# A reordered stage border, and token lists by one-hot products instead of scatters, in a scan layer with a top-1 expert layer behind it

## The reference

```
x = x + scan_layer(layernorm(x))
    dt    = softplus((x Wdt1^T) Wdt2^T + b)
    A_bar = exp(dt * A)                      # per token, column and state n
    B_bar = (A_bar - 1) / A * x * B_t[n]
    h     = A_bar * h + B_bar                # along the tokens
    y     = sum over n of h * C_t[n],  + D_skip * x
x = x + experts(layernorm(x))
    e   = argmax(softmax(x Wr + br))         # one of 8 per token
    out = gelu(x W1[e] + b1[e]) W2[e] + b2[e]
```

## Time and profile before

| | us |
|---|---|
| median of 3 runs | 740.08 (739.1 to 744.09) |
| the profiled execution, its own time | 739.52 |
| its span | 737.8 |
| PE busy | 683.1 (93%) |
| DVE busy | 545.9 (74%) |
| ACT busy | 470.5 (64%) |
| POOL busy | 472.8 (64%) |

### The profile page before, as it was taken

How to read it: one execution, slowest core, us unless ns; L and a number is a source line. 1 busy time by engine, 2 the same in 40 slices (tenths; PEclk the granted TensorE clock), 3 DMA queues, 4 the chain that set the end, 5 groups by cost and what they waited for, 6 DMA issues and landing times.

```text
span 737.8 us, 17452 instructions
## 1 busy us (share of the span) xinstructions
PE 683.1 (93%) x5820; PEld 575.8 (78%) x5821; DVE 545.9 (74%) x968; ACT 470.5 (64%) x983; POOL 472.8 (64%) x595
## 2 busy tenths in 40 slices
PE   8799899999998997997997887999999999999997
PEld 7677677787787776776776777889899999987776
DVE  5899999989999989998999997786433333344441
ACT  3986998998998987887895585322323233323451
POOL 3789988988969887899998684043324343333331
PEclk9699999999999998999999999999999999999999
DMA  7967843343242523372475379221111111211010
GB/s 241 303 205 266 270 153 83 114 149 115 89 140 92 152 86 104 67 142 87 85 148 60 74 215 310 82 65 44 52 56 51 54 56 45 64 31 39 26 44 14
DMA packets 43216, 82.46 MB, mean 112 GB/s; under 512 B 5368, under 2 KB 13565, under 8 KB 43136
## 3 DMA queue, kind: packets, MB, share of 16 engines
q1 hardware_dynamic: 38016, 68.84, 32.8%
q0 software_dynamic: 5120, 12.60, 5.7%
HBM read 69.49 MB, written 13.51 MB: 112 GB/s over the span
## 4 chain that ended last, share of the span: by engine, by line
PE 60%; ACT 13%; POOL 11%; issue 10%; DVE 3%; DMA 1%; DVEq 1%; POOLq 0%; ACTq 0%; SPq 0%
PE WW L1176 15%; PE misc L1213 15%; PE WW L1053 11%; POOL w_sb L667 7%; PE YY L1091 7%; ACT w_sb L842 5%; ACT Csb L832 5%; PE misc L1208 2%; PE WW L1170 2%; PE misc L971 2%; POOL b_sb L648 2%; PE misc L983 1%; DMA xin<-x_in 1%; PE YY L1139 1%; ACT xin L812 1%
## 5 line engine op out<-in xcount | busy, mean ns | idle before, releaser
L667 POOL TENSOR_TENSOR w_sb<-w_sb,Csb 128x512 f32<-128x512 f32 x202 | 255.3, 1275 | 53.2 <-DVE w_sb L1307 45.7
L1053 PE MATMUL WW<-b_sb,xin 64*128 64x130 f32 (+2 forms) x2304 | 202.3, 292 | 27.8 <-DVE w_sb L1307 14.5
L1053 PEld LDWEIGHTS WW<-b_sb,xin 64*128 64x128 f32 x2304 | 167.9, 191 | 74.7 <-issue 36.1
L1307 DVE TENSOR_TENSOR_SCAN w_sb<-WW,hlast,w_sb 128x512 f32<-128x512 f32 x152 | 187.6, 1268 | 7.0 <-PE WW L1053 4.2
L842 ACT ACTIVATE w_sb<-dt,negA 128x512 f32<-128x512 f32 x256 | 169.6, 709 | 8.4 <-DVE w_sb L1307 5.8
L918 ACT ACTIVATE dt<-WW,b1c 128x128 f32<-128x128 f32 x256 | 73.1, 387 | 137.0 <-PE WW L1176 132.5
L1091 PE MATMUL YY<-sm,w_sb 128*128 128x128 f32 x1024 | 143.0, 285 | 8.0 <-DVE row L1364 5.0
L740 POOL DMA_INDIRECT y_out<-CbX,ocol x36 | 42.2, 1171 | 157.8 <-DVE CbX L1732 153.4
L1091 PEld LDWEIGHTS YY<-sm,w_sb 128*128 128x128 f32 x1024 | 114.1, 144 | 22.8 <-issue 5.8
L1213 PE MATMUL misc<-w_sb,dt 128*128 x512 | 115.7, 379 | 0.4 <-issue 0.4
L832 ACT ACTIVATE Csb<-w_sb,invA 128x512 f32<-128x512 f32 x134 | 91.6, 713 | 28.9 <-POOL w_sb L667 28.7
(11 more groups left out here) (312 smaller groups left out, 828.1 us busy)
## 6 DMA issues: line engine op xcount, KB each, us to landing
w_sb<-c_rows SPq DMA_DIRECT2D x86, 256.0 KB, 4.0
CbX<-c_rows SPq DMA_DIRECT2D x42, 256.0 KB, 3.7
w_sb<-w_in SPq DMA_DIRECT2D x20, 512.0 KB, 6.4
token_rows<-row SPq DMA_DIRECT2D x8, 1024.0 KB, 4.9
w_sb<-w_in SPq DMA_DIRECT2D x24, 256.0 KB
xin<-x_in SPq DMA_DIRECT2D x8, 512.0 KB, 3.9
w_sb<-x_in SPq DMA_DIRECT2D x7, 512.0 KB, 7.8
b_sb<-b_in SPq DMA_DIRECT2D x1, 780.0 KB, 6.4
```

The source lines that it names most:

```text
L667: eng.tensor_tensor(hc[g % NHC], hb_of(g), Csb[i % NCS][:, :], ALU.mult).then_inc(s_hcp, 1)
L1053: return eng.matmul(to[:, a:a + width], x_rows[rows, k, h * P:(h + 1) * P], band[rows, k, at:at + width], start=start, stop=not start, ski ...
L1307: eng.tensor_tensor_scan(hb_of(g) if pooled(g) else w_of(g), w_of(g), A[g % NA], hlast[(q - 1) % 2][:, h * N + n:h * N + n + 1] if q % NC ...
```

## The change

It does three things.

1. VectorE's units change: in chunks 5 and 6 from 5, 8, 12 to 5, 12; in chunk 7 unit 13 becomes 15.
2. The early tiles' lists come from products of f32 marks. `mark_early(k)` writes two one-hot tiles for each of the 16 early tiles, 8 in chunk 5 and 8 in chunk 6, behind the scans of items 10, 12, ... 24. PE multiplies them in hops early0 (chunk 6) and early1 (chunk 7), in two halves each; `keep_half` and `keep_ids` store the sum. The scatters, the list in DRAM, its load and the hop `lists` are gone. `count` moves to the start.
3. The border is written in another order on DVE and PE, and ACT's first W1 copy moves into unit 12 of chunk 7.

The core of the diff:

```diff
-VECTOR_UNITS = [(1, 6, 9, 12)] + [(5, 8, 12)] * 6 + [(1, 4, 8, 10, 13)]
+VECTOR_UNITS = [(1, 6, 9, 12)] + [(5, 8, 12)] * 4 + [(5, 12)] * 2 + [(1, 4, 8, 10, 15)]
...
+        if q == NQ - 2:
+            at[1] = [("early0_a", q)] + at[1]
+            at |= {2: [("early0", q)]}
     else:
-        at = {1: [("cbt", q)], 3: [("u_a", q)], 4: [("u01", q), ("u23", q)], 6: [("lists", 0)],
+        at = {1: [("cbt", q)], 3: [("u_a", q)], 4: [("u01", q), ("u23", q)], 6: [("early1_a", q)], 7: [("early1", q)],
...
+        marks = w2_sb[:, 2 * H:4 * H].rearrange("p (j a c) -> p j a c", a=2, c=P)
...
                     if q == NQ - 1 and n == 9:
-                        load_lists()
-                    if 0 <= N * q + n - NB < 20:
+                        eng.wait_ge(s_full, HOP["early1", q] + 1)
+                        load_weights(18)
+                        load_weights(19)
+                    if 0 <= N * q + n - NB < 18:
...
-                    if q == NQ - 3 and n > 4 and n % 2:
-                        enlist(((n - 5) // 2,))
-                    if q == NQ - 2 and n % 2:
-                        enlist(((n + 11) // 2,))
-                    if last and n < 2:
-                        enlist((n + 14,))
...
+                    if last and n == 12:
+                        copy_first_W1()
...
-                elif name == "lists":
-                    eng.wait_ge(s_lists, 16 * (q + 1))
-                    for i in range(E * CAP // P):
-                        mm = eng.transpose(to[:, i * P:(i + 1) * P], lists_in[:, i * P:(i + 1) * P], ident)
+                elif name in ("early0", "early0_a", "early1", "early1_a"):
+                    group, half = int(name[5]), int(not name.endswith("_a"))
+                    for j in range(TI * half, TI * half + TI):
+                        eng.wait_ge(s_mark, 2 * TI * group + j + 1)
+                        mm = eng.matmul(to[:, 0:P], marks[:, j, 0, :], marks[:, j, 1, :], start=(j == 0),
+                                        stop=(j == 2 * TI - 1))
...
             def step(t, u, r):
-                if not (isinstance(t, int) and (t + 1 >= MT or t == 1)):
+                if not (isinstance(t, int) and (t + 1 >= MT or t in (1, 2))):
                     hidden(t + 1, (u + 1) % 4)
-                if not (isinstance(t, int) and t + 2 >= MT):
+                if not (isinstance(t, int) and (t + 2 >= MT or t == 1)):
                     turn_x(t + 2, (u + 2) % 4, r + (u + 2) // 4)
                 if isinstance(t, int) and t == 0:
+                    hidden(2, 2)
                     fill(*TAIL[0])
-                    hidden(2, 2)
-                    for hop in TAIL[1:5]:
+                    turn_x(3, 3, 0)
+                    for part in range(2):
+                        fill(*TAIL[1 + part])
+                        hidden(3, 3, (part,))
+                    for hop in TAIL[3:5]:
                         fill(*hop)
                         keep_warm(6)
+                outputs(t, u)
+                if isinstance(t, int) and t == 0:
                     fill("spread", 1)
-                outputs(t, u)
...
+            def mark_early(k):
+
+                if k == 2 * TI:
+                    eng.wait_ge(s_full, HOP["early0", NQ - 2] + 1)
+                j = k % (2 * TI)
+                eng.tensor_scalar(marks[:, j, 0, :], counted[:, 0:P], where[:, 0, k:k + 1], back[:, k:k + 1],
+                                  ALU.is_equal, ALU.mult)
+                eng.tensor_scalar(marks[:, j, 1, :].rearrange("p (e c) -> p e c", e=E),
+                                  counted[:, :].rearrange("p (e c) -> p e c", e=E)[:, :, 0:LEVELS],
+                                  where[:, 1, k:k + 1], None, ALU.is_equal).then_inc(s_mark, 1)
...
-                if batch == 0:
-                    eng.tensor_copy(slotu[:, :], slotf).then_inc(s_slot, 1)
-                    return
...
             def keep_ids():
 
-                eng.wait_ge(s_full, HOP["lists", 0] + 1)
-                eng.tensor_copy(ids[:, 0:E * CAP], spot("lists", 0)[:, 0:E * CAP]).then_inc(s_ids, 1)
+                eng.wait_ge(s_spread, 1)
+                eng.wait_ge(s_full, HOP["early1", NQ - 1] + 1)
...
+            def keep_half():
+
+                eng.wait_ge(s_full, HOP["early0", NQ - 2] + 1)
+                eng.tensor_scalar(listed0, spot("early0", NQ - 2)[:, 0:P], FAR, None, ALU.add).then_inc(s_spread, 1)
...
+                    if q in (NQ - 3, NQ - 2) and gap and j in range(10, 26, 2):
+                        mark_early((q - NQ + 3) * 2 * TI + (j - 10) // 2)
+                    if q == NQ - 2 and (j, gap) == (5, 0):
+                        keep_half()
...
             copy_W1(1, 1)
-            for part in range(4):
-                choose(1, part)
+            copy_W1(2, 2)
+            choose(1, 0)
             q = NQ - 1
             for i in range(2):
                 finish_rows(q, i)
             for i in range(2):
                 ln2_stats(i, q)
             aggregate(1, q)
-            eng.wait_ge(s_ids, 1)
-            count()
+            copy_xT(2, 2)
+            for part in range(1, 4):
+                choose(1, part)
+            copy_W1(3, 3)
+            copy_xT(3, 3)
...
                 if isinstance(t, int) and t == 0:
                     place_tokens(1)
+                    mark(1, range(0, 6))
                     logits(NQ - 1)
+                    mark(1, range(6, 12))
                     for part in range(4):
                         choose(2, part)
                     join(1)
```

108 lines of the change are left out of this document (51 added, 57 removed).

## The result

The changed kernel takes 745.5 us (median of 7 runs, 743.65 to 749.9), the kernel before 740.72 in the same comparison. The ratio is 1.0064, with a 95% interval of 1.0034 to 1.0095. The forecast was 746.9 us, 734 to 755. The profiled execution took 743.65 us, span 741.9 us, against 739.52: +4.13 us. Of the seven executions four lie at 743.65 to 745.5 us and three at 749.06 to 749.9, and the kernel before has two such groups too (739.1 to 740.72, and 744.09 to 744.58); both traces are of the faster group, and why there are two is not shown.

The account below looks back on a forecast made before the run. VectorE was taken to pace the chunks and TensorE the expert stage from 486 us. Terms 1.35 - 2.4 - 0.4 - 0.4 = -1.85 on 739.52 gave 737.7; plus 9.2 for engine exclusion, 746.9 us, range 734 to 755.

Parts of the forecast that it names:

- The price of taking turns: In chunks 5 and 6 VectorE's marks and GpSimd's products exclude each other for whole operations: +9.2 us with small steps.
- First operations: In chunks 5 and 6 a mark's first operation waits out a running GpSimd product: 3.5 us a chunk, 7.0 together.
- Second ones: In one mark of four a GpSimd product slips in before the mark's second operation: 2 a chunk, 5.1 us together.
- Idle time that marks and waits fell into: VectorE idle time in chunks 5 and 6 absorbs 1.0 us of marks and 1.5 us of waits in each.
- Chunk 5: Plain sum +1.35 us without exclusion: marks +3.7, small steps +0.65, unit 8 gone -1.6, TensorE waits -0.4, idle time -1.0.
- Chunk 6: Plain sum -2.4 us without exclusion: marks and keep_half add, unit 8, its wait, idle time and the x load's wait subtract.
- With the scatters gone I count those 3.1 as gained: In chunk 6 VectorE's 3.1 us idle around the slow x load disappears once list scatters are gone: -3.1 us.
- Chunk 7 and the border: Chunk 7 -0.4 us from lighter table and scatter work; border net -0.4 (ends -1.6 and +0.5), most earlier TensorE work not gained.
- The counting: Start work moved from the border to the kernel's beginning is hidden there and costs nothing; 1.5 us if not hidden.
- (a): VectorE and GpSimd hardly hinder each other, marks falling into pauses between products: 737.7 us, between 734 and 741; chance 0.22.
- (b): Every first mark operation and every second mark's other one waits for GpSimd: 756.3 us, up to 762; chance 0.11.
- (c): A clear gain: marks at 0.20 us an operation slip into VectorE's waits: 732.5 us, 728 to 733; chance 0.09.

Follow-up runs that it names:

- the PSUM operation: Changed kernel plus a small unread VectorE operation, 32 columns from PSUM to SBUF, ahead of 6 of 8 marks a chunk: 747.82 us, ratio 1.007.
- the SBUF one: Changed kernel plus a small unread VectorE operation, 32 columns from SBUF to SBUF, ahead of 6 of 8 marks a chunk: 755.02 us, ratio 1.0156.

## Why the prediction was right, step by step

**The price of taking turns** was the term on which the forecast stood (+9.2 us; without it 737.7), and it is there: marks and nothing else last 1.05 to 1.30 us, the PSUM operation beside them does not wait and the SBUF one does. Its size was too large. First operations: 3.5 us a chunk forecast, 2.4 measured. Second ones: two in eight forecast, one in eight measured, 1.0 us a chunk and not 2.5. Idle time that marks and waits fell into: 1.0 and 1.5 forecast, 2.9 measured in chunk 5. How many second operations lose their turn was a guess, and a good one by luck: shifted by one item, or by 0.2 us, they are five in eight.

**Chunk 5**: 1.35 + 4.6 = +5.95 forecast, +3.2 measured, by the two sizes just named. A mark's own 0.46 us were 0.43.

**Chunk 6**: -2.4 + 4.6 = +2.2 forecast, +2.35 measured, but right by luck, by two errors that cancel. The step that failed is "With the scatters gone I count those 3.1 as gained". The load did land in 3.7 us and not in 7.89, and TensorE's wait of 2.96 us fell to 1.68; yet VectorE stood 2.62 us in the same place before keep_half, which waits for the new hop early0. Nor were the 3.1 us the load's. VectorE's first wait, 1.32 us, ended at 342.80, before the load landed at 344.73, and it is 1.31 us with a load of 6.6 us. With the scatters in place and the load landing in 6.6 or 5.7 us, chunk 6 took 57.1 us, as against 57.2. The 3.1 us were not gained, and the price of the turns was lower by about as much.

**Chunk 7 and the border**: -0.4 - 0.4 forecast, -1.4 measured, which is +0.8 for chunk 7 and -2.2 behind it. VectorE's wait behind the early W1 copy was 0.78 us, where about 1.5 was forecast. The shape of the border was right: the wait before hidden(2) shrank to 0.90 us, the gap before the fifth tile's transposes came (4.6 forecast, 3.10 measured) and a slow outputs(2) behind it (1.2 forecast, 1.7 measured). The wait of outputs(1) for join(1), 1.39 us, was not seen: I had named join(1) as waiting for spread(1), and not asked who needs its bank next.

**The counting** was costed at nothing, "falls into the time in which VectorE has nothing but the first load to wait for". As a cost that is right. As an edit it is the best of the change, 0.54% by itself, since the 1.4 us left the queue ahead of copy_W1(2) just where TensorE waited, and in its trace no low clock followed. The forecast had this gain hidden in the border's sum, and gave the credit to the new order.

**The rivals.** (a) is out, by the PSUM and SBUF kernels. (b), the lock in full, did not come in this kernel, but in the one with the marks at odd items (5.4 us a chunk) it was near. (c) failed at its own condition: undisturbed marks do last 0.43 us a pair, the waits are what it lacked. The total is +4.1 in the profiled pair and +4.8 by the medians, against +7.4 in the sum: the right mechanism at half to two thirds of its size. That 745.5 lies so near 746.9 is in part luck, for the sum started from 739.52 and the kernel before had a median of 740.72 beside it.

**What stays open.** The parts don't add up. The lists cost 0.0110 on top of the counting (1.0056 against 0.9946), the new order 0.0048 on top of the counting (0.9994), but only 0.0008 on top of both. The intervals of 0.0025 on each side leave room for a difference of this size by chance, and no run here settles it. What grants TensorE the full clock behind one wait and the low one behind the same wait in another trace is open too.
